# A window attention kernel: the next image's inverse transforms move into the last two attention rows

## What is computed

```python
x = x + _L0_conv_ref(_gn(x), L0_conv_weight, L0_conv_alpha)      # 3x3 ternary convolution
x = x + _L1_conv_ref(_gn(x), L1_conv_weight)                     # spectral mixing: rfft2, 56 by 57 modes, irfft2
x = x + _L2_conv_ref(_gn(x), L2_conv_weight, L2_conv_bias)       # 7x7 convolution
x = x + _L3_conv_ref(_gn(x), ...)                                # 8x8 window attention, 8 heads, with a depthwise part
```

## Time and profile before

| | |
|---|---|
| median of 3 runs | 11730.43 us (11728.45 to 11733.97) |
| the profiled execution, its own time | 11728.25 us |
| its span | 11726.6 us |
| busy share of the span: PE, DVE, ACT, POOL | 87%, 68%, 52%, 34% |
| mean granted clock of TensorE | 0.928 of full speed |
| third stage, from its first product | 2820.0 us to 11726.6 us |
| mean distance of two images in it | 273.94 us (3049.41 to 11267.63, 30 images) |

### The profile page before, as it was taken

One profiled execution on the slowest core, in us unless ns is written; L12 is line 12 of the kernel. 1 busy time (PEld: TensorE's weight loads), 2 busy tenths in 40 slices (PEclk: granted clock), 3 DMA queues, 4 the chain that ended last, 5 costly groups with the idle time before them and its releaser, 6 DMA issues.

```text
span 11726.6 us, 292194 instructions
## 1 busy us (share of the span) xinstructions
PE 10203.8 (87%) x120871; PEld 9034.3 (77%) x120871; DVE 7999.6 (68%) x13647; ACT 6054.5 (52%) x7030; POOL 4027.2 (34%) x3437
## 2 busy tenths in 40 slices
PE   7999967774999998999999999999998999999996
PEld 5777767674888887888888888888887888888885
DVE  7777733335677777777777777777777777777775
ACT  4666631112555555555555555555555555555553
POOL 0000000003444444444444444444444444444442
PEclk9999987776999999999999999999999999999997
DMA  8999989982011111111111111111111111111100
GB/s 205 240 240 242 244 193 234 232 219 61 19 33 33 30 41 30 30 30 31 30 33 30 33 32 31 33 30 33 31 40 30 30 30 31 30 33 33 30 22 17
DMA packets 662368, 888.86 MB, mean 76 GB/s; under 512 B 479008, under 2 KB 594704, under 8 KB 637776
## 3 DMA queue, kind: packets, MB, share of 16 engines
q1 hardware_dynamic: 631120, 650.33, 25.0%
q0 software_dynamic: 29952, 220.22, 5.1%
HBM read 547.51 MB, written 322.96 MB: 74 GB/s over the span
## 4 chain that ended last, share of the span: by engine, by line
PE 38%; DVE 17%; issue 7%; ACT 7%; POOL 5%; DMA 1%; SPq 0%; DVEq 0%; POOLq 0%; ACTq 0%
PE c_ps L1078 23%; PE c_ps L1149 3%; POOL c_cube L1789 3%; PE c_ps L1227 2%; PE c_ps L1162 2%; PE c_ps L1214 2%; DVE c_v L1591 2%; ACT c_xp L1335 2%; DVE c_xp L1555 2%; DVE c_bn L1535 2%; DVE c_s L1654 2%; DVE c_xr L1573 2%; ACT c_sq L1398 1%; PE c_ps L1110 1%; DVE c_qt L1629 1%
## 5 line engine op out<-in xcount | busy, mean ns | idle before, releaser
L1078 PE MATMUL c_ps<-c_xp,c_wst 128*128 128x224 f16 x45696 | 4900.0, 265 | 154.8 <-DVE c_xp L1555 154.8
L1078 PEld LDWEIGHTS c_ps<-c_xp,c_wst 128*128 128x128 f16 x45696 | 4362.9, 98 | 626.8 <-issue 415.6
L1764 POOL TENSOR_TENSOR c_xr<-c_sm,c_xr 128x448 f32<-128x448 f32 x448 | 704.2, 1572 | 2221.8 <-DVE c_xr L1573 2221.8
L1789 POOL TENSOR_TENSOR c_cube<-c_sq,c_qk 128x896 f32<-128x896 f32 x448 | 928.4, 2094 | 1191.3 <-ACT c_sq L1389 1191.3
L1366 ACT ACTIVATE c_qt<-c_ps 128x896 f32<-128x896 f32 x224 | 205.9, 919 | 2040.5 <-PE c_ps L1170 2040.5
L638 PE MATMUL b_ps<-b_wt,b_xt 64*64 64x64 f32 x12768 | 730.0, 285 | 336.2 <-DVE b_xt L613 192.6
L1324 ACT ACTIVATE c_tn<-c_xr,c_nrm 64x448 f32<-64x448 f32 (+1 forms) x832 | 956.0, 1153 | 56.9 <-DVE c_xp L1555 27.0
L638 PEld LDWEIGHTS b_ps<-b_wt,b_xt 64*64 64x64 f32 x12768 | 711.7, 170 | 354.4 <-issue 354.0
L1149 PE MATMUL c_ps<-c_wqkv,c_xn 64*128 64x192 f32 x6272 | 790.3, 367 | 200.7 <-DVE c_v L1591 193.2
L1335 ACT ACTIVATE c_xp<-c_tn 128x1080 f16<-128x1080 f32 (+1 forms) x544 | 572.3, 1063 | 730.2 <-DVE c_tn L1548 726.4
L1555 DVE TENSOR_TENSOR c_xp<-c_tn,c_xp 128x1080 f16<-128x1080 f32 (+1 forms) x544 | 664.1, 1231 | 271.7 <-ACT c_xp L1335 270.7
(11 more groups left out here) (160 smaller groups left out, 17319.0 us busy)
## 6 DMA issues: line engine op xcount, KB each, us to landing
b_wt<-in_L_conv_weight SPq DMA_DIRECT2D x28, 4096.0 KB, 42.7
a_xc<-in_x SPq DMA_DIRECT2D x64, 1568.0 KB, 21.6
x<-a_x1s POOLq DMA_DIRECT2D x64, 1568.0 KB, 11.6
a_xh<-x SPq DMA_DIRECT2D x64, 1568.0 KB
c_xr<-x SPq DMA_DIRECT2D x224, 448.0 KB, 4.2
out<-c_xr SPq DMA_DIRECT2D x448, 224.0 KB, 3.1
b_xs<-xf SPq DMA_DIRECT2D x28, 2048.0 KB, 24.1
yf<-b_ys POOLq DMA_DIRECT2D x112, 512.0 KB, 9.8
```

The costliest lines, as they stand in the source:

```text
L1078: ins = pe.matmul(sums(c, p), wst[:, ws, pr, FIRST_TAP[p] + k].rearrange("p q o -> p (q o)"), xp[:, xs, PLANE[kind] + f, row:row + CROWS, ...
L1764: pool.tensor_tensor(here, apart(sm[:, half]).unsqueeze(1).to_broadcast([P, 2, CROWS, QW]), here, ALU.add).then_inc(s.added, 1)
L1789: pool.tensor_tensor(cube[:, :, k].rearrange("p q r c -> p r q c"), sq[:, :, :, k], qk[:, :, :, k], ALU.mult).then_inc(done, 1)
```

## The change

The third stage is no longer split into a turn and rows. The inverse transforms of image n+1 stand inside rows 5 and 6 of image n, and the last convolution chunk of image n is kept back, so that its 204 products stand behind row 6. Chunk 0 of the next image runs 112 products ahead of its row (`AHEAD`). `z` moves out of `xp` into a tile of its own and the memory of `tn`, so that each copy of a group becomes two; VectorE now makes five of the 16 copies, and three groups instead of four go by way of GpSimd. The ring is shifted for odd images (`ODD_AT`), and five instead of four plane chunks are made early. The last eighth of x1 is loaded into the memory of `ys` and moved to `xr` by a DMA later.

```diff
-PIECES = (14, 26, 38, 52, 72, 112, 188)
+PIECES = (14, 26, 38, 52, 72, 112, 188, 204)
+AHEAD = 112
+FIRST_STATS_AT = 70
+ROW5_PE = ((14, 0), (26, 0), (38, 0), (56, 0), (92, 0), (92, 2), (92, 10), (92, 12))
+ROW6_PE = ((14, 0, 0), (15, 0, 0), (16, 0, 0), (16, 2, 0), (16, 4, 0), (16, 8, 0), (16, 10, 72), (16, 12, 80))
+TURN_PE = (112, 180, 200)
+C1_DVE = (2, 5, 8, 11, 14)
+ROW5_C1, ROW6_C1 = (0, 1, 3, 4, 6, 7, 9, 10), (12, 13, 15)
+ROW5_TURNED, ROW6_TURNED = (2, 5, 8), (11, 14)
+ROW6_COPIES = ((0,), (1, 2), ())
+ROW6_X2 = ((0, 3, 0, 0), (3, 7, 0, 2), (7, 10, 2, 8), (10, 10, 8, 10))
+TURN_X2 = ((10, 12, 10, 10), (12, 14, 10, 14))
...
         @block.tensor
+                if more and a == A7 - 2:
+                    conv, c1 = ROW5_PE[i]
+                    conv_some(n, odd, more, min(AHEAD + CONV_MMS * a + conv, (A7 - 1) * CONV_MMS))
+                    first_inverse(n + 1, c1)
+                elif more and a == A7 - 1:
+                    c1, c2, conv = ROW6_PE[i]
+                    first_inverse(n + 1, c1)
+                    second_inverse(n + 1, c2)
+                    conv_some(n, odd, more, CONV_MMS * (A7 - 1) + conv)
...
+                if above_zero(n):
+                    conv_some(n, odd, more, FIRST_STATS_AT)
+                    stats(2 * n)
+                    conv_some(n, odd, more, AHEAD)
...
         @block.scalar
+                    act.activation(z_low[:, :, 4 * g:4 * g + 4].rearrange("p h o -> p o h"), got[:, :, 0:Z_LOW], ACT.Copy)
+                    act.activation(z_high[:, :, 4 * g:4 * g + 4].rearrange("p h o -> p o h"), got[:, :, Z_LOW:H], ACT.Copy
                                    ).then_inc(s.c1_taken, 1)
...
                 if a < A7 - 1:
                     window_rows(l + 1, a + 1, odd)
+                middle()
                 act.wait_ge(s.ratio_done, l + 1)
                 act.activation(fac[:], fac[:], ACT.Sqrt).then_inc(s.f_done, 1)
...
+                    if more and a == A7 - 2 and to:
+                        if len(to) > 1:
+                            take_c1(nxt, ROW5_C1[0:2])
...
+                        def end():
+                            if more and a == A7 - 2:
+                                take_c1(nxt, ROW5_C1[2:])
...
         @block.vector
+            def turn(n, odd, attention):
+                row, after = n * A7 - 1, 1 - odd
+                for part in TURN_X2:
+                    add_x2(n + 1, after, *part)
+                dve.wait_ge(s.x2_stats, (n + 2) * CHUNKS)
+                norm(0, 2 * n + 1, bn2)
+                padded_low(n + 1, after, 0)
+                padded_low(n + 1, after, 1)
+                if attention:
+                    divide(row)
+                    multiply(row)
+                    add_depthwise(row)
+                take_t(n, odd, A7 - 1, 3)
+                differ(n + 1, 0)
+                differ(n + 1, 1)
+                take_t(n, odd, A7 - 1, 4)
+                take_t(n, odd, A7 - 1, 5)
+                low_part(n + 1, after, 0)
+                padded_low(n + 1, after, 2)
+                low_part(n + 1, after, 1)
...
+                    elif more and a == A7 - 2:
+                        if at == 1:
+                            turn_c1(n + 1, ROW5_TURNED)
```

More of the change, by code:

```diff
@@ L1242, in last @@
+                if attention:
+                    numerator(row)
+                    conv_some(n, odd, more, turn + (TURN_PE[1] if more else CONV_MMS))
+                    turn_back(row)
+                    conv_some(n, odd, more, turn + (TURN_PE[2] if more else CONV_MMS))
+                    give_back(row)
+                conv_some(n, odd, more, A7 * CONV_MMS)
+            def last(n):
                 row = (n - 1) * A7
-                numerator(row - 1)
-                turn_back(row - 1)
@@ L1254, in last @@
                 give_back(row + A7 - 1)
-            image_steps(pe, B, bring, both, last)
+            image_steps(pe, B, start, image, last)
         @block.scalar
@@ L1412, in attend, with start @@
                                ).then_inc(s.dw_taken, 1)
-                high(1)
-            def both(n, odd, attention):
+                high(2)
+                end()
+            def start():
+                take_c1(0, [g for g in range(16) if g not in C1_DVE])
+                for i in range(len(COPIED)):
+                    copy_x2(0, i)
+                deviation(0)
+                for k in range(EARLY):
+                    padded_chunk(0, 0, k)
+                    high_part(0, 0, k)
@@ L1439, in last @@
                 turned(n * A7 - 1)
                 give(n * A7 - 1)
-            image_steps(act, B, bring, both, last)
+            image_steps(act, B, start, image, last)
         @block.vector
@@ L1698, in both @@
-                take_t(n, odd, A7 - 1, 8)
-                x3_stats(n, odd, A7 - 1)
-            def last(n, odd):
-                if above_zero(n * CHUNKS):
-                    dve.wait_ge(s.bn3_done, n * CHUNKS)
-                row = (n - 1) * A7
-                divide(row - 1)
-                multiply(row - 1)
-                add_depthwise(row - 1)
-                norm(1, 2 * n - 1, bn3)
-                for g in range(4):
-                    take_qkv(row, g)
-                relu(row)
+                    x3_stats(n, odd, A7 - 2)
@@ L1716, in last @@
                 add_depthwise(row + A7 - 1)
-            image_steps(dve, B, bring, both, last)
+            image_steps(dve, B, start, image, last)
         @block.gpsimd
```

751 lines of the change are left out of this document (460 added, 291 removed).

## The result

| | before | after |
|---|---|---|
| median | 11730.43 us (11728.45 to 11733.97) | 11669.92 us (11658.01 to 11685.25) |
| ratio, 95% interval | | 0.9949 [0.9935, 0.9964] |
| the profiled execution, its span | 11728.25, 11726.6 us | 11658.01, 11656.3 us |
| mean granted clock | 0.928 | 0.943 |
| mean distance of two images | 273.94 us | 271.36 us |

The change makes the kernel faster by 0.5%, 60 us. The forecast was 3%, 360 us; 11670 lies outside its range. What was forecast for rows 5 and 6 came out nearly. The rest did not: an image was to take 262.1 us and takes 271.4.

What follows compares the result with a forecast made beforehand. TensorE was taken as the bound, with gaps. Per image, 244.0 us of work, 15.1 of waits and 3.0 of slow clock made 262.1 for 273.94; over 30 images, with the ends, 11370 us, range 11130 to 11640.

Steps and rivals of the forecast that it cites:

- Row 5: TensorE's waits in row 5, mostly for ScalarE's and VectorE's copies of the first inverse's groups: 4.8 us an image.
- row 6: TensorE's waits in row 6, for VectorE's `take_qkv` and a ScalarE copy in the second inverse: 2.0 us an image.
- the next image's convolution: In the turn, TensorE waits 2.4 us while VectorE's path of 15.1 us outlasts 12.7 us of TensorE work.
- The prices of the pairs: Each pair of copies replacing one copy: 1.1 us on ScalarE (between 0.82 and 1.64), 0.7 on VectorE (0.57 to 1.14).
- The Trainium skill's rule on oscillation: Rival: clock falls at row 5, the turn and the second norm; image 266.9 us, 11511 us, chance 0.12.
- I take a third, 1.3: Rows 0 to 4: the ring's two wraps directly ahead of `kvm` cost 1.3 us an image, between 0 and 3.8.
- The third plane chunk, 1.1: In the turn it comes 5.4 us behind, against 5.0 of products; with odd images' wrap, 1.1 us on the mean.
- GpSimd's surcharge, 1.5: GpSimd's additions in the turn slowed beside VectorE's plane work: 1.5 us an image, between 0 and 3.8.
- the second `stats`: The second norm's `stats` wait for GpSimd's last sums of chunk 6: 1.2 us if GpSimd runs alone.
- The loop's branch: The branch falls every second image into a place where TensorE waits anyway: 0.5 us an image.
- The clock, 3.0: Slow clock per image: one fall of 2.6 us in row 5, 0.4 for the turn; ends 0 and 7.8.
- the rivals: Chances: waits covered 0.14, clock falling in three places 0.12, dear copies 0.12, no change 0.04, slower 0.08.

Runs made afterwards that it cites:

- pair_first: dummy16 with ScalarE's first two pairs of copies in row 5 ahead of `window_rows`, not behind it: 11362.51 us, 56 us slower than dummy16.
- kvm_first: The changed kernel with VectorE's second low part of a row written behind `kvm` instead of ahead of it: 11511.83 us, 158 us less.
- one_difference: kvm_load with VectorE's two differences of each full-height plane chunk made as one instruction: 11340.98 us, 81 us less than kvm_load.
- changed_two_edits: The changed kernel with low part behind `kvm` and one difference for two, the spectrum's load left in place: 11417.00 us, 253 less.
- load_later: The changed kernel with SyncE's load of the next spectrum moved from an image's end to row 2 of the next: 11609.00 us, 61 us less.
- kvm_load: kvm_first with the load of the next spectrum cut into four pieces, one in each of rows 1 to 4: 11421.93 us, 90 us less than kvm_first.
- dummy16: one_difference with 16 unused products more ahead of the wait for the third plane chunk: 11306.63 us, 34 us less than one_difference.
- out_late: one_difference with GpSimd's addition of the attention's output in the turn held until the third plane chunk is written: 11346.26 us, the same as one_difference.

## Why the prediction was wrong

**Right.** The picture of the kernel before: TensorE bound, what it loses are waits and clock, most of it in the turn. The change does what the walk said where one queue follows another. Row 5 waits for ScalarE's and VectorE's copies, 4.2 us for 4.8; row 6 1.5 for 2.0; the next image's convolution 2.08 for 2.4. The prices of the pairs were taken too high (0.71 to 0.77 us from start to start on ScalarE for 1.1, and so under the 0.82 that was called their least; 0.60 on VectorE for 0.7), which row 5 does not show, since its end hangs on the root and the scaling. Nothing in rows 5 and 6 used up the gain.

The Trainium skill's rule on oscillation (page "TensorE: Matmul & The Clock Gate", section "HAM oscillation — how this bites in real kernels"), by which waits between bursts of products let the clock fall and each burst pays anew, is borne out in part. In the changed kernel row 5's clock fell in 20 of 30 images, behind waits of 1.71 and 2.06 with work between, and the turn's in 26, behind the third chunk's wait; in pair_first row 5's fell in all 30, behind one wait of 4.03.

**Wrong, in the order of size.**

- *"I take a third, 1.3, since the rest of the row has slack."* The slack was TensorE's ahead of the product of k and v. What stands between the wraps and `kvm` is VectorE's queue, and that has none: it also waits 2.02 us there for ScalarE's high part. Waits of 3.5 us an image, and slow clock behind them: 151 us between the two stretches of 30 images, 158 in the medians (kvm_first). My upper bound for the two wraps was 3.8. The kernel before waited for kvm too, 50.7 us in its 30 images or 1.7 each, outside the row that I read.
- *The third plane chunk, 1.1, and GpSimd's surcharge, 1.5.* The surcharge exists, but here it is VectorE's. The earlier trace rows showed GpSimd's additions at 2.32 beside plane work, and I charged it there. In those rows VectorE's instruction is under way first and keeps its time (1.29). In the turn GpSimd's first addition starts 0.13 us ahead of VectorE's difference, and VectorE is the one that waits. The order of the two starts is what I did not ask for. The third chunk costs 5.7 us of VectorE more in an image with a wrap, and TensorE waits 4.4 us for it on the mean; the second `stats`, where I had put the 1.5 and 1.2, wait for nothing. One instruction fewer for each chunk gave 81 and 95 us (one_difference; changed_two_edits against kvm_first).
- *"The loop's branch falls every second image into a place where TensorE waits anyway: 0.5."* Behind the branch an engine stops until instructions have come, and the load of the spectrum, which the change puts in the same microseconds and for which the sum has no term, makes the stop long. 1.6 us an image in waits, with its clock 61 to 90 us in all (load_later, kvm_load). The kernel before had such stops too, on TensorE itself: 2.6 to 3.0 us in 13 of its 30 images, 1.2 an image.
- *The clock, 3.0: one fall in row 5 at 2.6, 0.4 for the turn.* Measured are 5.6, and the other way round: row 5's falls come to about 1.1 an image (20 of 30, 1.7 us each), the rest lies in the turn and the rows behind it. I counted the falls from a forecast of waits that was too short there. What a few falls fewer are worth by themselves is 33 us (dummy16).

The edits against the first three bring the changed kernel to 11341 us, near the forecast's 11370. That is in part luck: they also take off what the forecast had left in (wraps 1.3, branch 0.5, part of the third chunk), and two of them save 46 us in the kernel before. On equal terms the change is worth 268 us where 360 were forecast. So the gain was taken back mostly by waits that were already in the forecast as terms, each sized by a guess at its cover.

The working had upper bounds for three of its terms: 3.8 for the wraps (taken 1.3), 3.8 for GpSimd (1.5) and 7.8 for the clock (3.0). With all three the image is 262.1 + 2.5 + 2.3 + 4.8 = 271.7, against 271.4 measured. This agreement is chance, since the clock took 5.6 and not 7.8, and the planes 6.5 for 3.5. What holds is that the rivals let the terms grow one at a time, and the range ended below their joint case; but they can go together, since a wait can bring a slow clock behind it.

Two things stay open: why out_late gains nothing, and the 92 us between the 268 and the 360.

## What to carry to other kernels

A wait in the bounding engine is priced by the queue of the engine that ends it: list what that engine does between the ready input and the release, its own waits included, and ask of each instruction there whether it could stand behind the release. When a change lays two engines' SBUF work over each other, ask which of the two will be under way first: in the old trace it can be the other one that pays. When it lays a long load over a loop's turn, look in the old trace for stops there that nothing releases, and expect them to grow. And if a large change moves the time little, remove its new waits one at a time: here two edits of VectorE's queue and one of a load turned 0.5% into 3.3%, and 16 useless products made it 3.6%.
